# Attention block and feed-forward on one core: y turned by VectorE's 32x32 blocks and DRAM, new instruction orders

## The chip, the cores and the metric

The kernel runs on 1 core of one Trainium2 chip. The metric is the device time of one execution in microseconds (us), the slowest core's, which here is the only one; lower is better. TensorE, VectorE, ScalarE and GpSimd compute, SyncE issues DMAs. The profile calls them PE (PEld is its weight load), DVE, ACT, POOL and SP.

## What is computed

```python
x = x + layernorm(attention(layernorm(x), Wqkv, Wo))          # x is 32 batches of 256 x 128
x = x + layernorm(tanh(layernorm(x) @ w @ aux1 @ aux2 + bias))
# attention: 8 heads of 64; q and k get a positional table; causal softmax in float32
```

Below, y is the layernorm of the first sum (x1), the input of the feed-forward. All tensors are float32. The three feed-forward matrices are multiplied once, at the start, into wf.

## The kernel before

Every engine has one fixed list of instructions, written out in Python and unrolled: `begin()`, then two slots for each batch (`slot(b, 0)` and `slot(b, 1)`), then `end()`. `all_slots` (L197) calls them for batches 0 to 30; batch 31 is in `end()`. Engines meet by semaphores only, so an instruction whose semaphore isn't reached holds up everything behind it on its engine. Slots of different engines that have the same number don't run at the same time: each list says by `b.plus(n)` which batch it works on. The 8 heads are 4 pairs, named by k (half, 0 or 1) and j (pair in the half).

One batch goes through these steps:

- x: loaded (`load_x`, L218), statistics on VectorE (`stats_x`), normalised by GpSimd (`norm_x`: var_eps, rstd, minus mean, times rstd). VectorE turns its 32x32 blocks (`turn_x_blocks`, L750), SyncE sends them in four DMAs to a DRAM tensor, so placed that the whole is transposed (`send`, L240), and reads it back (`read_x`, L255). ScalarE rounds it (`keep_x_hi`, L367), VectorE takes the rest (`keep_x_lo`, L740). Batch 0 alone is transposed on TensorE.
- QK of each pair: six matmuls into the one qk_bank (`make_qk`, L974 to L976), out of which VectorE adds the positional table (`keep_qk`, L705).
- Scores (`make_scores`, L956), masked maximum on VectorE (`row_max`, L695), exp with row sums on ScalarE (`exps`, L323), reciprocal (`invert_sums`, L711). The probabilities are scaled by ScalarE (k 0, j 0), VectorE (k 1, j 0) and GpSimd (j 1, L484).
- Turning (`turn_probs`, L999) transposes the probabilities on TensorE; ScalarE keeps them (`keep_turned`, L352, L354). Both halves use the same banks.
- Vals (`make_vals`, L942 to L944) fill misc_bank, kept by ScalarE (`keep_vals`, L344). Heads (`make_heads`, L1013) are kept by VectorE (`keep_heads`, L730). Attention output (`make_attn`, L1076) uses the left half of misc_bank and is kept by ScalarE (`keep_attn`, L392).
- VectorE takes statistics and moments of the attention output, GpSimd its rstd, VectorE normalises (`norm_attn`, L679), GpSimd adds x (`make_x1`, L546), VectorE takes y's statistics and moments, GpSimd normalises y (`norm_y`, L471, L473).
- y: TensorE transposes it into the right half of misc_bank (`turn_y`, L1019), ScalarE copies it to yt (`keep_y`, L375), TensorE makes the feed-forward of it (`make_ffn`, L1047, L1049), ScalarE takes tanh (L383). The last layernorm and sum are GpSimd's (`norm_ffn`, `make_out`, L530), and SyncE stores (L261).

misc_bank is shared by vals, attention output, y and feed-forward, so each waits until the other was kept. In `end()` TensorE has `warm_up` matmuls (L1106) whose results nothing uses; 12 of them stand between the feed-forward of batch 30 and the transposes of the last y.

## Time and profile before

| | us |
|---|---|
| median of 3 runs (lowest, highest) | 536.49 (535.29, 536.52) |
| the profiled execution | 535.58 |
| its span, first to last instruction | 533.3 |
| busy PE | 508.7 (95%) |
| busy PEld | 419.7 (79%) |
| busy DVE | 458.1 (86%) |
| busy ACT | 434.5 (81%) |
| busy POOL | 394.7 (74%) |

All times in the text are of the profiled execution, from the span's start. Busy time is the time in which an engine runs at least one instruction; a pipelined matmul's end is modelled, so groups that follow each other overlap in the rows, and the distance of their starts is the better measure. In a row the instruction's start comes first, then its duration; "x12" merges twelve; in brackets stands the idle time before it and what released it.

### The profile page before, as it was taken

The numbers are of one execution on the slowest core, as the hardware profiler recorded it, in microseconds if no ns is written. First come the engines' busy times: TensorE is split into PE (matmuls) and PEld (weight loads), VectorE is DVE, ScalarE is ACT, GpSimd is POOL, SyncE is SP. The second block draws the span as 40 slices with busy tenths as digits, with TensorE's granted clock in tenths as the row PEclk, the third lists the DMA queues.
The fourth block names the chain that finished last, engine by engine and source line by source line (L and its number), as shares of the span: only waits on it lengthen the run. The fifth ranks groups of instructions, "written<-read, shape, count | busy, mean of one in ns | idle before, by whom it ended". The sixth has DMA issues, their size and how long they took to land.

```text
span 533.3 us, 17276 instructions
## 1 busy us (share of the span) xinstructions
PE 508.7 (95%) x5334; PEld 419.7 (79%) x5334; DVE 458.1 (86%) x2062; ACT 434.5 (81%) x1604; POOL 394.7 (74%) x650
## 2 busy tenths in 40 slices
PE   7689999999999999999999999999999999999984
PEld 4578888888888888888888888888888888888762
DVE  4779889988889998888999988889998889998744
ACT  2698888988888888988888888888888888889731
POOL 4434578877777887777788777778878777886654
PEclk9899999999999999999999999999999999999989
DMA  5111122111211211121121112212111221210000
GB/s 157 41 41 42 26 47 51 33 46 47 51 42 40 53 32 48 44 50 45 39 52 40 41 42 53 52 31 52 45 39 42 51 51 31 53 40 12 22 21 20
DMA packets 66223, 23.52 MB, mean 44 GB/s; under 512 B 35923, under 2 KB 65622, under 8 KB 66134
## 3 DMA queue, kind: packets, MB, share of 16 engines
q1 hardware_dynamic: 65174, 21.71, 16.9%
q8 instruction: 44, 0.72, 0.6%
q10 hardware_dynamic: 960, 0.72, 0.4%
q14 instruction: 45, 0.37, 0.3%
HBM read 14.16 MB, written 8.26 MB: 42 GB/s over the span
## 4 chain that ended last, share of the span: by engine, by line
PE 85%; issue 3%; ACT 3%; POOL 3%; DVE 3%; DMA 2%; SPq 1%; POOLq 0%; DVEq 0%; ACTq 0%
PE turned_and_heads L1013 16%; PE scores L956 15%; PE misc_bank L1076 11%; PE turned_and_heads L999 11%; PE qk_bank L974 7%; PE qk_bank L975 5%; PE qk_bank L976 5%; PE misc_bank L942 3%; PE misc_bank L943 2%; PE misc_bank L1049 2%; PE misc_bank L944 2%; PE misc_bank L1019 2%; PE misc_bank L1047 1%; DMA xt<-x_rows 1%; ACT probs L323 1%
## 5 line engine op out<-in xcount | busy, mean ns | idle before, releaser
L323 ACT ACTIVATE probs<-scores,neg_max 128x256 f32<-128x256 f32 (+1 forms) x512 | 210.2, 437 | 15.3 <-DVE neg_max L695 14.9
L695 DVE CUSTOM_DVE_ANT_0 scores<-scores,mask 128x256 f32<-128x256 f32 (+1 forms) x512 | 164.9, 385 | 7.3 <-PE scores L956 7.1
L323 ACT ACTIVATION_READ_ACCUMULATOR probs<-scores,neg_max 128x1 f32 x512 | 113.5, 222 | 0.0
L484 POOL TENSOR_TENSOR probs<-probs,inv_sum 128x512 f32<-128x512 f32 x126 | 102.8, 837 | 11.1 <-DVE inv_sum L711 11.1
L352 ACT COPY pt<-turned_and_heads 128x512 f32<-128x512 f32 x128 | 75.4, 589 | 37.8 <-PE turned_and_heads L999 37.4
L956 PE MATMUL scores<-qk 64*128 64x256 f32 (+1 forms) x1024 | 100.0, 335 | 1.1 <-ACT probs L323 1.1
L1013 PE MATMUL turned_and_heads<-pt,vals 128*64 128x256 f32 (+1 forms) x1024 | 98.5, 335 | 0.3 <-ACT pt L354 0.2
L1013 PEld LDWEIGHTS turned_and_heads<-pt,vals 128*64 128x64 f32 x1024 | 64.4, 138 | 34.7 <-issue 12.8
L956 PEld LDWEIGHTS scores<-qk 64*128 64x128 f32 x1024 | 84.7, 190 | 8.0 <-issue 1.3
L705 DVE TENSOR_TENSOR qk<-qk_bank,pe 128x512 f32<-128x512 f32 x128 | 85.7, 669 | 4.4 <-PE qk_bank L976 4.2
L974 PE MATMUL qk_bank<-xt_hi,w_hi 128*128 128x256 f32 x256 | 81.3, 318 | 4.2 <-DVE qk L705 3.4
L999 PE MATMUL turned_and_heads<-ident,probs 64*128 64x64 f32 x1536 | 75.1, 229 | 3.9 <-ACT pt L354 2.7
L999 PEld LDWEIGHTS turned_and_heads<-ident,probs 64*128 64x128 f32 x1536 | 59.6, 138 | 15.9 <-issue 11.0
L975 PE MATMUL qk_bank<-xt_lo,w_hi 128*128 128x256 f32 x256 | 71.9, 281 | 0.0
L976 PE MATMUL qk_bank<-xt_hi,w_lo 128*128 128x256 f32 x256 | 71.9, 281 | 0.0
L695 DVE DVE_READ_ACCUMULATOR2_ANT neg_max<- 128x1 f32 x512 | 69.8, 136 | 0.0
L1076 PE MATMUL misc_bank<-wo,heads_t 128*128 128x128 f32 x496 | 62.6, 279 | 3.8 <-issue 0.6
L1076 PEld LDWEIGHTS misc_bank<-wo,heads_t 128*128 128x128 f32 x496 | 57.7, 191 | 9.0 <-issue 9.0
L974 PEld LDWEIGHTS qk_bank<-xt_hi,w_hi 128*128 128x128 f32 x256 | 48.2, 188 | 14.2 <-issue 9.1
L730 DVE COPY heads_t<-turned_and_heads 128x512 f32<-128x512 f32 x64 | 44.3, 692 | 6.8 <-PE turned_and_heads L1013 4.6
L975 PEld LDWEIGHTS qk_bank<-xt_lo,w_hi 128*128 128x128 f32 x256 | 48.3, 189 | 1.3
L354 ACT COPY pt<-turned_and_heads 128x256 f32<-128x256 f32 x128 | 48.8, 381 | 0.0
(95 smaller groups left out, 905.3 us busy)
## 6 DMA issues: line engine op xcount, KB each, us to landing
x_in<-in_x SPq DMA_DIRECT2D x32, 128.0 KB, 2.3
x_res<-in_x SPq DMA_DIRECT2D x32, 128.0 KB, 2.2
out_x<-x SPq DMA_DIRECT2D x32, 128.0 KB, 2.3
x_rows<-x_blocks SPq DMA_DIRECT2D x124, 32.0 KB, 2.0
xt<-x_rows SPq DMA_DIRECT2D x31, 128.0 KB, 2.6
w_raw<-in_w_qkv_t SPq DMA_DIRECT2D x2, 256.0 KB, 4.5
w_raw<-in_w_qkv_t ACTq DMA_DIRECT2D x1, 256.0 KB, 4.4
pe<-pe_table SPq DMA_DIRECT2D x1, 256.0 KB, 5.5
```

The lines of the kernel that those rows point to most:

```text
L323: ins = nc.scalar.activation(probs[k][j][:, h, lo:hi], s_bank[j][:, h, lo:hi], ACT.Exp, bias=neg_max[k][j][:, i:i + 1], scale=-1.0, accum_ ...
L352: nc.scalar.copy(pt0[j][:, :, :].rearrange("p h (n f c) -> p (h n) f c", n=2, f=2), turned_banks[:, :, 0:T].rearrange("p f (n c) -> p n f ...
L484: ins = nc.gpsimd.tensor_tensor(some, some, inv, ALU.mult)
L695: ins = nc.vector.tensor_tensor_reduce(some, some, mask[:, t * P:2 * P], -1.0, HIGHEST, ALU.add, ALU.min, neg_max[k][j][:, i:i + 1])
L705: nc.vector.tensor_tensor(qk[j][:, :], qk_bank[:, :], pe[:, :], ALU.add).then_inc(qk_kept, 1)
L956: ins = mm(s_bank[j][:, h, at:at + k_hi], qk[j][r, q_lo:q_lo + P], qk[j][r, T:T + k_hi], start=(at == 0), stop=True, skip_group_check=True)
L974: mm(to, w_hi[:, f], hi[:, :], start=True, stop=False)
L975: mm(to, w_hi[:, f], lo[:, :], start=False, stop=False)
L976: ins = mm(to, w_lo[:, f], hi[:, :], start=False, stop=True)
L999: ins = nc.tensor.transpose(turned_banks[:, f, n * D:(n + 1) * D], some[r, h, lo:lo + P], ident[r, r])
L1013: ins = mm(heads_bank[h * D:(h + 1) * D, to], vals[b.parity][:, s, f:f + D], rhs[j][:, h, :], start=(s == 0), stop=(s == 1))
L1076: ins = mm(misc_bank[:, t * E:(t + 1) * E], heads_t[b.parity][:, p, t * P:(t + 1) * P], wo[:, p, :], start=(p == 0), stop=(p == PAIRS - 1))
```

## The change

y is no longer transposed by TensorE and copied by ScalarE. VectorE turns its 32x32 blocks (`turn_y_blocks`) from yn into y_blocks, SyncE sends them in four DMAs to a DRAM tensor y_rows (`send_y`) and reads the whole back to yt (`read_y`). Only the last batch's y goes by TensorE as before (`turn_y_last`, `keep_y_last`). The feed-forward of batch b stands one slot later in TensorE's list; it waits for y_moved and for the kept attention output of batch b + 1. All engines' slots and ends have new orders. Batches 0 to 2 have lists of their own in `begin()`, so `all_slots` starts at batch 3. In them batch 1's x too is transposed by TensorE (`turn_x`), and on VectorE the statistics of batch 1 come ahead of the first weight rest. SyncE's read_x moves to the first slot, behind both sends; load_res comes later, and each batch has 5 more DMAs.

The diff, cut (indentation shortened by twelve):

```diff
@@ all_slots
-for b in range(0, 4):
+for b in range(3, 4):
     for k in range(2):
         slot(Batch(b // 2, b % 2, B), k)
@@ sync: send_x, read_x, send_y, read_y, slot
 def send_x(b):
-    if not b.exists() or b.is_below(1):
-        return
-    sp.wait_ge(x_blocked, b.times(1))
+    if not b.exists() or b.is_below(2):
+        return
+    sp.wait_ge(x_blocked, b.times(1, -1))
     send(b, x_blocks, x_rows, x_sent)
 def read_x(b):
-    if not b.exists() or b.is_below(1):
-        return
-    sp.wait_ge(x_sent[b.parity], moves(b, 1) * 64)
+    if not b.exists() or b.is_below(2):
+        return
+    sp.wait_ge(x_sent[b.parity], moves(b, 2) * 64)
     sp.dma_start(xt[b.parity][:, :, :], x_rows[b.parity]).then_inc(x_moved[b.parity], 16)
+def send_y(b):
+    if not b.exists() or not b.plus(1).exists():
+        return
+    sp.wait_ge(y_blocked, b.times(1, 1))
+    send(b, y_blocks, y_rows, y_sent)
+def read_y(b):
+    if not b.exists() or not b.plus(1).exists():
+        return
+    sp.wait_ge(y_sent[b.parity], moves(b, 0) * 64)
+    sp.dma_start(yt[b.parity][:, :], y_rows[b.parity].rearrange("p t e -> p (t e)")).then_inc(y_moved[b.parity], 16)
 def store(b):
     if not b.exists():
...
 def slot(b, k):
     if k == 0:
         load_x(b.plus(3))
+        read_y(b.plus(-3))
+        load_res(b.plus(-1))
         send_x(b.plus(2))
+        send_y(b.plus(-2))
+        read_x(b.plus(2))
     else:
-        read_x(b.plus(2))
         store(b.plus(-3))
-        load_res(b.plus(1))
@@ scalar: keep_x_hi, keep_y, slot
 def keep_x_hi(b):
     if not b.exists():
         return
-    if b.is_first():
-        act.wait_ge(x_turned, 1)
+    if b.is_below(2):
+        act.wait_ge(x_turned, b.times(1, 1))
     else:
-        wait_moved(act, b, x_moved, 1)
+        wait_moved(act, b, x_moved, 2)
     wait(act, qk_made, pairs(b, -2, 0))
     wait(act, vals_made, b.times(2, -2))
-    nc.scalar.copy(xt_hi[b.parity][:, :], misc_bank[:, 0:T] if b.is_first() else turned_x(b)
+    nc.scalar.copy(xt_hi[b.parity][:, :], misc_bank[:, 0:T] if b.is_below(2) else turned_x(b)
                    ).then_inc(x_hi_kept, 1)
-def keep_y(b):
...
+def keep_y_last():
+    act.wait_ge(y_turned, 1)
+    act.wait_ge(ffn_made, B - 2)
+    nc.scalar.copy(yt[1][:, :], misc_bank[:, T:2 * T]).then_inc(y_kept, 1)
 def slot(b, k):
     if k == 0:
-        tanh(b.plus(-3))
+        keep_vals(b.plus(-1), 0)
+        exps(b.plus(-1), 1, 1)
+        keep_turned(b.plus(-1), 0, 0)
+        keep_vals(b.plus(-1), 1)
+        keep_turned(b.plus(-1), 0, 1)
         exps(b, 0, 0)
         keep_attn(b.plus(-2))
         exps(b, 0, 1)
+        keep_x_hi(b.plus(1))
+        keep_turned(b.plus(-1), 1, 0)
+        scale_probs(b)
     else:
-        keep_x_hi(b.plus(1))
-        scale_probs(b)
-        keep_turned(b.plus(-1), 1, 0)
-        keep_vals(b, 0)
+        tanh(b.plus(-3))
         keep_turned(b.plus(-1), 1, 1)
         exps(b, 1, 0)
-        keep_vals(b, 1)
-        exps(b, 1, 1)
-        keep_turned(b, 0, 0)
-        keep_y(b.plus(-2))
-        keep_turned(b, 0, 1)
...
@@ gpsimd: norm_y, slot
-    wait(pool, y_turned, b.times(1, -1))
+    wait(pool, y_blocked, b.times(1, -1))
 def slot(b, k):
     if k == 0:
+        rstd_attn(b.plus(-2))
         make_x1(b.plus(-2))
         norm_x(b.plus(2))
         norm_y(b.plus(-2))
+    else:
         scale_probs(b, 0)
-    else:
         norm_ffn(b.plus(-3))
         make_out(b.plus(-3))
         scale_probs(b, 1)
-        rstd_attn(b.plus(-1))
@@ gpsimd: end
 def end():
+    rstd_attn(last.plus(-2))
     make_x1(last.plus(-2))
     norm_y(last.plus(-2))
     scale_probs(last, 0)
     norm_ffn(last.plus(-3))
+    make_out(last.plus(-3))
+    rstd_attn(last.plus(-1))
+    make_x1(last.plus(-1))
+    norm_y(last.plus(-1))
     norm_ffn(last.plus(-2))
-    rstd_attn(last.plus(-1))
-    make_out(last.plus(-3))
-    make_x1(last.plus(-1))
     make_out(last.plus(-2))
-    norm_y(last.plus(-1))
     rstd_attn(last)
     rstd_y(last)
     norm_ffn(last.plus(-1))
     make_out(last.plus(-1))
     rstd_ffn(last)
 all_slots(pool, slot, begin, end)
@@ vector: turn_y_blocks, slot
+def turn_y_blocks(b):
+    if not b.exists() or not b.plus(1).exists():
+        return
+    dve.wait_ge(norms["y"]["normed"], b.times(1, 1))
+    if not b.is_below(2):
+        wait_moved(dve, b.plus(-2), y_moved, 0)
+    nc.vector.transpose(y_blocks[b.parity][:, :, :], yn[b.parity][:, :, :]).then_inc(y_blocked, 1)
 def slot(b, k):
     if k == 0:
+        scale_probs(b.plus(-1))
+        stats_x(b.plus(2))
+        turn_y_blocks(b.plus(-3))
+        row_max(b, 0, 0)
         invert_sums(b.plus(-1), 1, 1)
-        row_max(b, 0, 0)
         row_max(b, 0, 1)
         keep_qk(b, 1, 0)
-        stats_ffn(b.plus(-3))
+        wait_stats("x", b.plus(2))
         stats_attn(b.plus(-2))
+        take_moments("x", b.plus(2))
+        wait_stats("attn", b.plus(-2))
+        keep_heads(b.plus(-1), 0)
+        take_moments("attn", b.plus(-2))
         invert_sums(b, 0, 0)
-        wait_stats("attn", b.plus(-2))
-        stats_x(b.plus(2))
-        take_moments("attn", b.plus(-2))
     else:
-        wait_stats("x", b.plus(2))
-        keep_heads(b.plus(-1), 0)
-        take_moments("x", b.plus(2))
+        keep_qk(b, 1, 1)
         norm_attn(b.plus(-2))
-        keep_qk(b, 1, 1)
-        invert_sums(b, 0, 1)
         keep_x_lo(b.plus(1))
+        row_max(b, 1, 0)
         stats_y(b.plus(-2))
         wait_stats("y", b.plus(-2))
-        row_max(b, 1, 0)
+        invert_sums(b, 0, 1)
         take_moments("y", b.plus(-2))
+        stats_ffn(b.plus(-3))
         keep_qk(b.plus(1), 0, 0)
         row_max(b, 1, 1)
+        wait_stats("ffn", b.plus(-3))
         invert_sums(b, 1, 0)
-        wait_stats("ffn", b.plus(-3))
+        take_moments("ffn", b.plus(-3))
         keep_heads(b.plus(-1), 1)
-        take_moments("ffn", b.plus(-3))
         turn_x_blocks(b.plus(2))
         keep_qk(b.plus(1), 0, 1)
-        scale_probs(b)
@@ vector: begin, first part
 def begin():
     stats_x(first)
-    wait_stats("x", first)
-    take_moments("x", first)
+    moments("x", first)
     norm_first()
+    stats_x(first.plus(1))
+    moments("x", first.plus(1))
     take_w_rest(0)
     keep_x_lo(first)
     take_w_rest(1)
-    stats_x(first.plus(1))
-    wait_stats("x", first.plus(1))
-    take_moments("x", first.plus(1))
     take_w_rest(2)
-    dve.wait_ge(pe_in, 16)
     keep_qk(first, 0, 0)
+    stats_x(first.plus(2))
+    moments("x", first.plus(2))
+    keep_x_lo(first.plus(1))
     keep_qk(first, 0, 1)
     keep_fused(0)
+    row_max(first, 0, 0)
+    keep_qk(first, 1, 0)
+    row_max(first, 0, 1)
     keep_fused(1)
-    turn_x_blocks(first.plus(1))
-    dve.wait_ge(mask_in, 16)
+    keep_qk(first, 1, 1)
+    invert_sums(first, 0, 0)
+    stats_x(first.plus(3))
+    turn_x_blocks(first.plus(2))
+    row_max(first, 1, 0)
+    invert_sums(first, 0, 1)
+    keep_qk(first.plus(1), 0, 0)
...
@@ tensor: make_vals, make_ffn, slot
+    if b.is_below(3) and t == 0:
+        wait(pe_eng, vals_kept, b.times(2))
+    if b.is_first() and t == 0:
+        pe_eng.wait_ge(w_hi_made, 3)
+        pe_eng.wait_ge(w_lo_made, 3)
     if t == 0:
         wait(pe_eng, attn_kept, b.times(1, -1))
         wait(pe_eng, tanh_done, b.times(1, -2))
-        pe_eng.wait_ge(x_lo_kept, b.times(1, 1))
-        wait(pe_eng, y_kept, b.times(1, -2))
+        pe_eng.wait_ge(x_lo_kept, 2 if b.is_first() else b.times(1, 1))
     else:
         pe_eng.wait_ge(vals_kept, b.times(2, 1))
     hi, lo = xt_hi[b.parity][:, t * P:(t + 1) * P], xt_lo[b.parity][:, t * P:(t + 1) * P]
...
-    pe_eng.wait_ge(y_kept, b.times(1, 1))
+    if b.plus(1).exists():
+        wait_moved(pe_eng, b, y_moved, 0)
+    else:
+        pe_eng.wait_ge(y_kept, 1)
+    if b.plus(2).exists():
+        pe_eng.wait_ge(attn_kept, b.times(1, 2))
+    else:
+        pe_eng.wait_ge(attn_kept, B - 1)
+        pe_eng.wait_ge(tanh_done, b.times(1))
     mm(misc_bank[:, T:2 * T], part_ones[:, :], bias_parts[:, :], start=True, stop=False, skip_group_check=True)
 def slot(b, k):
     if k == 0:
-        make_qk(b, 1, 1)
-        turn_probs(b.plus(-1), 1, 0)
-        make_scores(b, 1)
-        turn_probs(b.plus(-1), 1, 1)
-        make_qk(b.plus(1), 0, 0)
-        make_vals(b, 1)
-        make_heads(b.plus(-1), 1)
-        make_qk(b.plus(1), 0, 1)
-    else:
-        turn_y(b.plus(-2))
-        turn_probs(b, 0, 0)
-        make_scores(b.plus(1), 0)
-        turn_probs(b, 0, 1)
-        make_ffn(b.plus(-2))
-        make_qk(b.plus(1), 1, 0)
         make_attn(b.plus(-1), 0)
         make_attn(b.plus(-1), 1)
+        make_qk(b.plus(1), 1, 0)
         make_heads(b, 0)
+        make_qk(b.plus(1), 1, 1)
+        turn_probs(b, 1, 0)
+        make_scores(b.plus(1), 1)
+        turn_probs(b, 1, 1)
+    else:
+        make_ffn(b.plus(-2))
+        make_qk(b.plus(2), 0, 0)
         make_vals(b.plus(1), 0)
+        make_heads(b, 1)
+        make_qk(b.plus(2), 0, 1)
+        make_vals(b.plus(1), 1)
+        turn_probs(b.plus(1), 0, 0)
+        make_scores(b.plus(2), 0)
+        turn_probs(b.plus(1), 0, 1)
@@ tensor: begin, first part
+    turn_x(first)
     warm_up(7, qk_bank)
     make_qk(first, 0, 0)
-    pe_eng.wait_ge(w_hi_made, 3)
-    pe_eng.wait_ge(w_lo_made, 3)
+    turn_x(first.plus(1))
+    make_qk(first, 0, 1)
+    fuse(0)
+    make_scores(first, 0)
+    make_qk(first, 1, 0)
+    fuse(1)
     make_vals(first, 0)
-    make_qk(first, 0, 1)
-    pe_eng.wait_ge(ffn_in, 16 * 3)
-    fuse(0, w2_sb, w1t_sb)
-    make_scores(first, 0)
-    pe_eng.wait_ge(fused_dve, 1)
-    fuse(1, w12t_sb, w3_sb)
-    make_qk(first, 1, 0)
+    make_qk(first, 1, 1)
+    make_vals(first, 1)
+    make_scores(first, 1)
+    make_qk(first.plus(1), 0, 0)
+    turn_probs(first, 0, 0)
+    make_qk(first.plus(1), 0, 1)
+    make_vals(first.plus(1), 0)
+    turn_probs(first, 0, 1)
+    make_scores(first.plus(1), 0)
+    make_qk(first.plus(1), 1, 0)
...
@@ tensor: end
 def end():
-    turn_probs(last.plus(-1), 1, 0)
-    make_qk(last, 1, 1)
-    make_vals(last, 1)
-    turn_probs(last.plus(-1), 1, 1)
-    make_scores(last, 1)
-    make_heads(last.plus(-1), 1)
-    turn_y(last.plus(-2))
-    turn_probs(last, 0, 0)
-    make_ffn(last.plus(-2))
-    turn_probs(last, 0, 1)
     make_attn(last.plus(-1), 0)
     make_attn(last.plus(-1), 1)
     warm_up(4, qk_bank, 256)
     make_heads(last, 0)
     warm_up(4, qk_bank, 256)
     turn_probs(last, 1, 0)
+    make_ffn(last.plus(-2))
     turn_probs(last, 1, 1)
     warm_up(4, qk_bank, 256)
     make_heads(last, 1)
     pe_eng.wait_ge(exps_done, 4 * B)
     warm_up(3, s_bank[0][:, 0, :])
     make_attn_last()
-    turn_y(last.plus(-1))
     make_ffn(last.plus(-1))
     warm_up(12, s_bank[0][:, 0, :])
-    turn_y(last)
+    turn_y_last()
     warm_up(4, s_bank[0][:, 0, :], 256)
     make_ffn(last)
 all_slots(pe_eng, slot, begin, end)
```

## Rows read from the trace of the kernel before

**Rows 1.** Busy time in one batch: us; PE, PEld, DVE, ACT, POOL; PEclk, DMA, GB/s.
```profile
265.46:280.92 15.46, 15.34 (x167) 12.86 (x165) 14.05 (x65) 13.45 (x51) 12.43 (x20) 1.00 0.19 45
```

**Rows 2.** Timeline of PE from 271 to 281 us.
```profile
271.65 0.28 PE L976 MATMUL qk_bank<-xt_hi,w_lo 128*128 128x256 f32 x1
271.77 0.44 PE L1019 MATMUL misc_bank<-ident,yn 128*128 128x128 f32 x2
272.14 0.59 PE L999 MATMUL turned_and_heads<-ident,probs 64*128 64x64 f32 x12
...
275.62 0.28 PE L976 MATMUL qk_bank<-xt_hi,w_lo 128*128 128x256 f32 x1
276.03 2.02 PE L1076 MATMUL misc_bank<-wo,heads_t 128*128 128x128 f32 x16
277.98 1.52 PE L1013 MATMUL turned_and_heads<-pt,vals 128*64 128x256 f32 x16
...
280.00 0.39 PE L944 MATMUL misc_bank<-w_hi,xt_lo 128*128 128x512 f32 x1
280.23 0.28 PE L974 MATMUL qk_bank<-xt_hi,w_hi 128*128 128x256 f32 x1
```

**Rows 3.** Timeline of PE in the first 60 us.
```profile
17.98 0.36 PE L974 MATMUL qk_bank<-xt_hi,w_hi 128*128 128x256 f32 x1 [3.16 <-DVE qk L705]
...
40.66 0.56 PE L999 MATMUL turned_and_heads<-ident,probs 64*128 64x64 f32 x11
...
55.21 0.59 PE L999 MATMUL turned_and_heads<-ident,probs 64*128 64x64 f32 x12
```

**Rows 4.** Timeline of POOL and PE in the last 20 us.
```profile
518.36 0.20 POOL L461 TENSOR_TENSOR y_var_eps<-y_moments,eps 128x2 f32<-128x2 f32 x1 [3.03 <-DVE y_moments L644]
...
522.31 2.75 PE L1106 MATMUL scores<-warm 128*128 128x512 bf16 x12
...
525.90 0.44 PE L1019 MATMUL misc_bank<-ident,yn 128*128 128x128 f32 x2 [0.83 <-DVE yn L808]
```

**Rows 5.** Timeline of PE from 499 to 507 us.
```profile
499.27 0.40 PE L944 MATMUL misc_bank<-w_hi,xt_lo 128*128 128x512 f32 x1
499.60 0.59 PE L999 MATMUL turned_and_heads<-ident,probs 64*128 64x64 f32 x12
...
505.79 0.59 PE L999 MATMUL turned_and_heads<-ident,probs 64*128 64x64 f32 x12 [0.47 <-ACT pt L354]
506.31 0.94 PE L1076 MATMUL misc_bank<-wo,heads_t 128*128 128x128 f32 x6
```

**Rows 6.** Timeline of DVE and of POOL from 262.5 to 275 us.
```profile
263.96 0.23 DVE L644 BATCH_NORM_AGGREGATE attn_moments<-attn_stats 128x2 f32<-128x6 f32 x2
...
271.67 1.61 POOL L484 TENSOR_TENSOR probs<-probs,inv_sum 128x512 f32<-128x512 f32 x2
```

**Rows 7.** Waits of DVE (total us, times, longest), and its 31 block transposes.
```profile
DVE attn_stats L631 <- ACT attn L392: 24.9, 31, 1.1
DVE attn_n L679 <- POOL attn_rstd L464: 10.8, 31, 0.7
...
L750 DVE STREAM_TRANSPOSE x_blocks<-xn 128x256 f32<-128x256 f32 x31 | 12.8, 414 | 0.0
```

**Rows 8.** DMA issues, landing of xt's reads, and SP's four sends.
```profile
x_rows<-x_blocks SPq DMA_DIRECT2D x124, 32.0 KB, 2.0
...
DMA to landing us min/median/max: 1.9/2.6/4.2
...
272.32 2.55 SPq L240 DMA_DIRECT2D x_rows<-x_blocks  x4
```

**Rows 9.** Timeline of DVE and of ACT in the first 22 us.
```profile
8.85 0.49 DVE L631 BATCH_NORM_STATS2 x_stats<-x_in 128x6 f32<-128x128 f32 x2 [0.69 <-DMA x_in<-in_x]
...
20.90 0.41 ACT L367 CAST xt_hi<-xt 128x256 fp32r<-128x256 f32 x1 [1.50 <-DMA xt<-x_rows]
```

**Rows 10.** The page's costliest groups: exps on ACT (busy us, mean ns, idle before).
```profile
L323 ACT ACTIVATE probs<-scores,neg_max 128x256 f32<-128x256 f32 (+1 forms) x512 | 210.2, 437 | 15.3 <-DVE neg_max L695 14.9
```

262 lines of the change are left out of this document (200 added, 62 removed).

## The prediction

> **What bounds the kernel now.** I read the page's busy shares first, then the busy time of one batch, then TensorE's instructions over one batch, then the waits, and last the first 60 and the last 30 us. TensorE leads with 95% of the span (the table above), and within one batch of the middle it is busy 15.34 of 15.46 us at full granted clock [rows 1]. What the reader is to see in its timeline [rows 2] is that each group starts where the one before it ends: a batch lasts 15.47 us, and from the first turning of batch 2 (55.21) [rows 3] to that of batch 16 (272.14) a batch takes 216.93 / 14 = 15.50 us, hiccups included. So in the middle only TensorE's own list counts, unless another chain becomes as long. VectorE is next: 14.05 us of a batch [rows 1], plus the waits it cannot avoid. The ends are different: TensorE stands idle there, and chains set the time [rows 3, 4].
>
> **Steady state, TensorE's list.** A batch keeps the same groups, less the two transposes of y. They cost no more than their place in the list: from the last matmul of the first half's second QK group (271.65) to the transposes 0.12 us, from them to the next turning 0.37 [rows 2]. Neighbours change too, so I count each step from a group's last matmul (or its start, where its length does not change) to the next group. Steps that go: QK to turned y 0.12, turned y to turning 0.37, QK to attention output 0.41 (276.03 less 275.62), vals to QK 0.23 (280.23 less 280.00) [rows 2]; sum 1.13. Steps that come: vals to turning, 0.33, and turning to attention output, 0.52, within the 0.59 that a turning itself lasts, so nothing is lost there [rows 5]. QK to heads and QK to the first half of vals have no row. Each has three waits; QK to a group whose wait is over costs 0.12, QK to attention output with its four waits 0.41. I take 0.25 for each, between the two, as three waits are nearer to four than to none but at least one is long over. So 1.13 is replaced by 0.33 + 0.50 = 0.83: 0.30 less a batch, 15.20 us. Bounds 0.56 less (both 0.12) and 0.02 more (both 0.41).
>
> **Steady state, the chains beside it.** The new lists are tight, so I follow three loops. (1) Heads of the first half, kept by VectorE 1.57 us after they begin (length 1.52 and a hand-over of 0.05) [rows 2], 0.61 of VectorE until the moments of the attention output, then from those moments through rstd, norm_attn, x1, norm_x and norm_y to GpSimd's scaling 7.71 (263.96 to 271.67), the scaling 1.61, turning 0.52, attention output 1.95, QK 0.8 and 0.25: 15.0 us [rows 2, 5, 6]. Before, this chain hung on the attention output and had about 0.6 to spare; now it hangs on the heads and is 0.2 short of TensorE. (2) VectorE: 14.05 + 0.41 for turning y's blocks + the wait inside its own list between the moments and norm_attn, 10.8 / 31 = 0.35: 14.8 us [rows 1, 7]. Its other wait, 24.9 / 31 = 0.8 for the kept attention output [rows 7], must shrink to what is left, 0.4. (3) The round trip of y. SyncE issues 13 DMAs a batch instead of 8. An issue of send takes 0.65 (2.55 for four), so its queue fills about 7.5 us, with read_x now behind both sends and read_y behind store and load_x. From VectorE's turn: 0.41, four issues 2.6, flight 2.0, read 2.6 = 7.6 us until y has moved [rows 7, 8]. The room for it: VectorE keeps the heads 1.57 after they begin; of its 14.8 us the turn of y, two row maxima, a kept QK, one stats, one moments and one inversion (0.36 + 2.5 + 0.6 + 0.4 + 0.2 + 0.1 = 4.1) lie between that turn and the next heads, so the turn is 1.57 + 10.7 = 12.3 after the heads' start. The feed-forward is 4.8 after the heads of its slot (heads 1.45, QK 1.0, turning 0.42, scores 1.38, turning 0.52), so 15.2 + 4.8 - 12.3 = 7.7 us after the turn. The trip just fits, and what is late by e costs e/2 a batch, since this loop spans two batches. ScalarE loses y's copy, but is busy 13.45 only and gains nothing for the end. With all three loops within 0.1 to 0.4 of TensorE's 15.20 I take 15.30 a batch: 0.20 less, over the 27 batches from 3 to 29, **-5.3 us**. From -10 (15.13) to +1.
>
> One rule speaks against moving a transpose off TensorE: the Trainium skill, "VectorE: DVE Perf Modes", Rules for kernel authors, would leave a 128x128 transpose on TensorE where PSUM may take it. The rows above say that here TensorE has no room and VectorE has 0.4 us, so the rule would give 0 for the steady state and my sum -5.3.
>
> **The start.** Now the first turning of batch 1 is at 40.66 [rows 3]. TensorE idled 3.16 us up to 17.98, because VectorE took both row maxima before it kept a QK [rows 3], and batch 1's x came by DRAM, with ScalarE idle 1.50 for it [rows 9]. The new lists put a keep_qk between the maxima and turn batch 1's x on TensorE. Against that, VectorE's statistics of batch 1 now stand ahead of the first weight rest. Their data lands at 8.85 only [rows 9], so the first QK result is kept some 2 us later than now, at about 12.2. From there I walk the lists: first scores 13.8 to 15.3, their first row maximum 14.8 to 16.0, exps to 17.7 (four activations of 0.437 mean, overlapping to 1.6) [rows 10], then a kept half of vals, the second exps 18.2 to 19.8 behind its maximum, scaling 1.5, first turning 21.9. Then ScalarE holds the pace: exps of the second half to 23.4, keep_turned 0.75, exps to 25.8, so the next scores end at 26.5; behind them QK, heads, vals, QK, turning, scores, turning, QK, a short wait for keep_turned (33.7), heads, QK, half an attention output and scores follow (0.9 + 1.5 + 0.7 + 0.8 + 0.5 + 1.4 + 0.5 + 0.8 + 0.2 + 1.5 + 0.8 + 1.0 + 1.4 = 12.0) to 38.5 for the turning of batch 1. One score group (1.4) and half an attention output (1.0) are by then done that now come later: 40.66 + 2.4 - 38.5 = 4.6 gained. A walk has no friction; I take **-3.8**. Bounds -5 and +1 (nothing gained but the late start kept).
>
> **The end.** y of batch 30 must cross DRAM too, and in TensorE's list its feed-forward and 12 warm-up matmuls stand ahead of the last y. Its moments were taken late (GpSimd idle 3.03 until 518.36) [rows 4]; now they are taken at once and GpSimd normalises it earlier, so I put the normed y at 516.5. Add 7.6 for the trip: 524.1, 0.6 of feed-forward and 2.6 of warm-up (2.75 with the last one's tail, from 522.31): the last y is turned at 527.3 instead of 525.90, +1.4 [rows 4]. The front of the tail gains 0.4 (one turning of y less). **+1.0**, from -0.5 to +2.7.
>
> **Sum.** The profiled execution took 535.58 us with 533.3 us of span. 535.58 - 5.3 - 3.8 + 1.0 = 527.5 us. The median of the runs, 536.49, is 0.9 above the profiled one; I do not add that. A change under 0.3% (1.6 us) is about what a measurement of this kernel cannot tell from none.
>
> **Rivals.** (A) *The steps on TensorE cost what the old ones did*: the waits of heads and vals show in full (0.41 each), or TensorE waits 0.2 for keep_heads, now only one QK behind the heads. The middle stays at 15.50, start and end as above: 532.8 us. For it: the loops leave 0.2. 20%. (B) *y is late, slower than before*: feed-forward waits for y's read in every batch. It decides from the point where the loop of two batches passes 31.0 + 0.2, that is where y comes some 0.9 us later than forecast. The sends of x and y now share the rings, and both sends and the read could be slower: reads landed after 1.9 to 4.2 us [rows 8]. With 1.5 us more the batch is 15.15 + 0.75 = 15.9: 27 x 0.4 = +10.8, with start and end 543.5 us. Against it: 32 KB sends land in 2.0 us, less than a 128 KB read. 12%. The Trainium skill, "DMA: Bandwidth & Descriptors", Why small descriptors are slow (HBM only), names small pieces as slow, and y's sends are made of them. The same send of x lands in 2.0 us in the row, so the trace so far does not bear the rule out. (C) *VectorE becomes the bound*: its extra 0.41 and a worse fit of waits (it has 0.4 us) eat the middle's gain and 2 us of the start: 535 us, no difference. 10%. (D) *No loop binds and the new steps cost 0.12*: 15.1 a batch, 522 us. 8%. The forecast itself: 50%, its own range 524 to 531.
>
> Faster: forecast, A, D = 0.78. Same: C = 0.10. Slower: B = 0.12. The range goes from 523, which leaves out most of D, to 536, which leaves out B.
>
> **What would show it.** In the changed profile the two transposes of y are gone from the middle, the vals to turning step is 0.33 and QK to heads and to vals about 0.25. First turnings of successive batches are 15.3 us apart. VectorE is busy 14.4 us of that, and 31 turns of y's blocks of 0.41 stand there. TensorE's longest releaser in the middle is none, or VectorE's kept heads. A wait of feed-forward for the DMA of y of more than 0.3 us a batch means B. The first turning of batch 1 near 38.5, the last y turned 1 to 1.5 us later within the tail. A period over 15.45, or a start later than 41, would make the forecast wrong.

## The result and the profile after

| | us |
|---|---|
| kernel after, median of 7 runs (lowest, highest) | 538.63 (535.86, 541.39) |
| kernel before, beside it, 7 runs | 536.12 (534.65, 536.69) |
| ratio, 95% interval | 1.0048 [1.0026, 1.0070] |
| profiled execution after, and its span | 536.81, 534.6 |

The change makes the kernel 0.5% slower, where I forecast 527.5 us. The profiled execution is 1.8 us below the median: it is a good one of its kind, and this matters below.

The page of the kernel after: busy times, packets, and the chain that ended last (shares of the span by engine).

```profile
PE 502.0 (94%) x5274; PEld 413.6 (77%) x5274; DVE 470.8 (88%) x2092; ACT 427.6 (80%) x1573; POOL 395.3 (74%) x650
DMA packets 103184, 31.40 MB, mean 59 GB/s; under 512 B 69043, under 2 KB 102582, under 8 KB 103094
PE 51%; DVE 16%; SPq 9%; issue 8%; DMA 7%; ACT 5%; POOL 3%; POOLq 0%; DVEq 0%; ACTq 0%
```

TensorE has 6.7 us less work than before (508.7), as meant, and yet the end comes no earlier. The last line tells why: it held 85% of the chain before and holds 51% now, and SyncE's queue and DMAs, 3% before, have 16%. Something on SyncE is now in the way.

One batch of the middle, in the columns of [rows 1]: it lasts longer than one before (15.46), but TensorE is busy for 15.07 of it, not 15.34 (15.08 of 15.64 in the batch ahead of it).

```profile
271.57:287.39 15.82, 15.07 (x164) 12.62 (x163) 14.43 (x66) 13.21 (x52) 12.75 (x21) 1.00 0.28 60
```

The same batch on four engines. VectorE turns x's blocks and, 2.7 us later, y's:

```profile
270.83 0.44 DVE L812 STREAM_TRANSPOSE x_blocks<-xn 128x256 f32<-128x256 f32 x1
...
273.57 0.42 DVE L821 STREAM_TRANSPOSE y_blocks<-yn 128x256 f32<-128x256 f32 x1
```

SyncE issues what follows from that, one thing behind the other:

```profile
271.30 2.55 SPq L242 DMA_DIRECT2D x_rows<-x_blocks  x4
274.02 3.85 SPq L242 DMA_DIRECT2D y_rows<-y_blocks  x4
277.92 0.60 SPq L257 DMA_DIRECT2D xt<-x_rows  x1
```

ScalarE waits for x, and TensorE for the copy that stands behind that wait:

```profile
280.28 0.41 ACT L386 CAST xt_hi<-xt 128x256 fp32r<-128x256 f32 x1 [1.34 <-DMA xt<-x_rows]
280.60 0.58 ACT L371 COPY pt<-turned_and_heads 128x512 f32<-128x512 f32 x1
```

```profile
279.54 1.56 PE L1086 MATMUL scores<-qk 64*128 64x256 f32 x16
281.70 0.59 PE L1129 MATMUL turned_and_heads<-ident,probs 64*128 64x64 f32 x12 [0.60 <-ACT pt L373]
```

The last of x's four sends is issued at 273.24 and landed at 275.22. Their read is issued at 277.92, because y's four sends are ahead of it in the queue. Over the run it looks like this (waits: total us, times, longest):

```profile
ACT xt_hi L386 <- DMA xt<-x_rows: 16.7, 20, 1.4
...
PE turned_and_heads L1129 <- ACT pt L373: 6.9, 13, 1.2
...
PEld misc_bank L1180 <- DMA yt<-y_rows: 6.0, 8, 3.9
```

Before, the first of these waits was 1.9 us, twice. The middle as a whole is read from the first turning of batch 3 and that of batch 30, before and after:

```profile
70.59 0.28 PE L999 MATMUL turned_and_heads<-ident,probs 64*128 64x64 f32 x2
...
489.15 0.28 PE L999 MATMUL turned_and_heads<-ident,probs 64*128 64x64 f32 x2
```

```profile
69.83 0.28 PE L1129 MATMUL turned_and_heads<-ident,probs 64*128 64x64 f32 x2
...
488.77 0.28 PE L1129 MATMUL turned_and_heads<-ident,probs 64*128 64x64 f32 x2
```

27 batches took 418.56 us and take 418.94: 15.50 and 15.52 each. The start gained 0.76 in these two profiles. The tail, from the turning of batch 30 to the end of the span, took 533.3 - 489.15 = 44.15 and takes 534.6 - 488.77 = 45.83: 1.7 lost.

The start, which I had put 3.8 us faster. VectorE waits for batch 1's x with the weights' rests behind it, so the first QK comes at 10.86; then TensorE waits for that x again, with the second QK behind it:

```profile
9.13 0.49 DVE L689 BATCH_NORM_STATS2 x_stats<-x_in 128x6 f32<-128x128 f32 x2 [3.49 <-DMA x_in<-in_x]
```

```profile
10.86 0.39 PE L1104 MATMUL qk_bank<-xt_hi,w_hi 128*128 128x256 f32 x1 [2.71 <-DVE xt_lo L802]
...
13.22 0.33 PE L1149 MATMUL misc_bank<-ident,xn 128*128 128x128 f32 x1 [1.07 <-POOL xn L520]
...
24.33 0.28 PE L1129 MATMUL turned_and_heads<-ident,probs 64*128 64x64 f32 x2
...
41.69 0.28 PE L1129 MATMUL turned_and_heads<-ident,probs 64*128 64x64 f32 x4
```

The tail: y of batch 30 is sent and read, TensorE waits for it, and 12 warm-up matmuls stand between its feed-forward and the last y. They take 3.65 us now and took 2.75 before [rows 4]: behind the wait of 3.68 us TensorE was granted half its clock, 1.2 GHz, for 3.4 us (0.77 and 0.81 in the two windows of 4 us, third from the end of the row; 1.00 in both before).

```profile
516.09 2.54 SPq L242 DMA_DIRECT2D y_rows<-y_blocks  x4
...
520.73 0.34 SPq L272 DMA_DIRECT2D yt<-y_rows  x1
```

```profile
522.70 0.40 PE L1180 MATMUL misc_bank<-bias_parts,part_ones 128*128 128x256 bf16 x1 [3.68 <-DMA yt<-y_rows]
...
523.74 3.65 PE L1238 MATMUL scores<-warm 128*128 128x512 bf16 x12
527.22 0.38 PE L1149 MATMUL misc_bank<-ident,yn 128*128 128x128 f32 x2
```

```profile
520.00:524.00 4.00, 1.30 (x6) 1.14 (x7) 1.77 (x7) 0.02 (x1) 1.69 (x4) 0.77 0.21 66
524.00:528.00 4.00, 4.00 (x18) 1.83 (x16) 1.26 (x6) 0.73 (x2) 2.24 (x5) 0.81 0.00 0
```

### The profile page after: what moved, and what is told of

Its sections match the earlier page's. It is cut to its first block, busy times and chain, and to the rows that moved or that the text cites. A ratio compares the mean times of both kernels' runs of the same rounds, so it can differ in the third digit from the quotient of the medians.

```text
span 534.6 us, 17330 instructions
## 1 busy us (share of the span) xinstructions
PE 502.0 (94%) x5274; PEld 413.6 (77%) x5274; DVE 470.8 (88%) x2092; ACT 427.6 (80%) x1573; POOL 395.3 (74%) x650
## 4 chain that ended last, share of the span: by engine, by line
PE 51%; DVE 16%; SPq 9%; issue 8%; DMA 7%; ACT 5%; POOL 3%; POOLq 0%; DVEq 0%; ACTq 0%
PE turned_and_heads L1143 11%; SPq L242 8%; PE scores L1086 8%; PE misc_bank L1209 7%; PE turned_and_heads L1129 7%; DMA xt<-x_rows 4%; PE qk_bank L1104 4%; DVE scores L755 4%; PE qk_bank L1105 3%; PE qk_bank L1106 3%; DVE qk L767 2%; PE misc_bank L1182 2%; PE misc_bank L1072 2%; DVE probs L783 2%; PE misc_bank L1073 2%
## 5 line engine op out<-in xcount | busy, mean ns | idle before, releaser
L531 POOL TENSOR_TENSOR probs<-probs,inv_sum 128x512 f32<-128x512 f32 x126 | 111.1, 902 | 20.3 <-DVE inv_sum L773 20.3
L342 ACT ACTIVATION_READ_ACCUMULATOR probs<-scores,neg_max 128x1 f32 x512 | 117.8, 230 | 0.0
L1143 PE MATMUL turned_and_heads<-pt,vals 128*64 128x256 f32 (+1 forms) x1024 | 97.3, 332 | 0.9 <-ACT pt L373 0.7
L1086 PEld LDWEIGHTS scores<-qk 64*128 64x128 f32 x1024 | 87.8, 190 | 4.7 <-issue 0.8
L1129 PE MATMUL turned_and_heads<-ident,probs 64*128 64x64 f32 x1536 | 75.2, 229 | 13.5 <-ACT pt L373 6.9
L1104 PE MATMUL qk_bank<-xt_hi,w_hi 128*128 128x256 f32 x256 | 84.0, 328 | 3.6 <-DVE xt_lo L802 2.7
L755 DVE DVE_READ_ACCUMULATOR2_ANT neg_max<- 128x1 f32 x512 | 71.0, 139 | 0.0
L1209 PE MATMUL misc_bank<-wo,heads_t 128*128 128x128 f32 x496 | 63.7, 281 | 0.1
L783 DVE TENSOR_TENSOR probs<-probs,inv_sum 128x512 f32<-128x512 f32 x64 | 49.3, 809 | 0.1
```

Of the source, the lines that this page charges most:

```text
L342: ins = nc.scalar.activation(probs[k][j][:, h, lo:hi], s_bank[j][:, h, lo:hi], ACT.Exp, bias=neg_max[k][j][:, i:i + 1], scale=-1.0, accum_ ...
L531: ins = nc.gpsimd.tensor_tensor(some, some, inv, ALU.mult)
L755: ins = nc.vector.tensor_tensor_reduce(some, some, mask[:, t * P:2 * P], -1.0, HIGHEST, ALU.add, ALU.min, neg_max[k][j][:, i:i + 1])
L1086: ins = mm(s_bank[j][:, h, at:at + k_hi], qk[j][r, q_lo:q_lo + P], qk[j][r, T:T + k_hi], start=(at == 0), stop=True, skip_group_check=True)
L1104: mm(to, w_hi[:, f], hi[:, :], start=True, stop=False)
L1129: ins = nc.tensor.transpose(turned_banks[:, f, n * D:(n + 1) * D], some[r, h, lo:lo + P], ident[r, r])
```

## The experiments

All are edits of the kernel after. "Period" is the distance of the first turnings of batches 3 and 30 in the profiled execution, divided by 27. Ratios are to runs of the kernel before made beside them (medians 535.5 to 536.1).

| run | median us | ratio [95%] | period |
|---|---|---|---|
| no_trip | 530.82 | 0.9902 [0.9876, 0.9928] | 15.33 |
| trip_unused | 537.28 | 1.0033 [1.0015, 1.0050] | 15.52 |
| x_hi_later | 544.43 | 1.0157 [1.0131, 1.0182] | 15.74 |
| start_stats_later | 539.62 | 1.0067 [1.0045, 1.0089] | 15.65 |
| x_turn_earlier | 539.76 | 1.0071 [1.0049, 1.0093] | 15.55 |
| plain_sends | 532.35 | 0.9936 [0.9913, 0.9959] | 15.34 |
| tail_warm_first | 538.11 | 1.0046 [1.0025, 1.0067] | 15.67 |
| start_x1_later | 539.71 | 1.0067 [1.0044, 1.0090] | 15.62 |
| sp_order | 535.16 | 0.9990 [0.9968, 1.0012] | 15.42 |
| y_read_first | 539.39 | 1.0068 [1.0047, 1.0089] | 15.51 |
| start_warm | 540.94 | 1.0091 [1.0060, 1.0121] | 15.75 |
| all_three | 533.07 | 0.9955 [0.9935, 0.9976] | 15.36 |
| no_trip_scale_first | 525.68 | 0.9805 [0.9788, 0.9822] | 15.15 |
| three_scale_first | 531.80 | 0.9915 [0.9890, 0.9940] | 15.43 |
| three_start | 530.74 | 0.9893 [0.9873, 0.9912] | 15.45 |
| three_act_send | 530.30 | 0.9888 [0.9872, 0.9905] | 15.33 |
| all_one_send | 525.45 | 0.9794 [0.9771, 0.9816] | 15.26 |
| all_two_sends | 531.59 | 0.9913 [0.9894, 0.9932] | 15.44 |

Four of these runs leave the middle as it is in the kernel after (start_stats_later, tail_warm_first, start_x1_later, start_warm). Their profiles show 15.62 to 15.75, but these executions took 0.5 to 3.6 us more than the medians of their own runs, as the one with 15.52 took 1.8 less. If all of that lay in the middle, the five would come to 15.57 to 15.62 (an estimate). Without the trip it is 15.33, in an execution 0.3 above its median. So periods of single profiles tell differences of 0.2, but hardly of 0.1.

**no_trip**: the trip taken out, the blocks used as they are.

```diff
 def slot(b, k):
-    read_y(b.plus(-3))
-    send_y(b.plus(-2))
...
-    wait_moved(pe_eng, b, y_moved, 0)
+    pe_eng.wait_ge(y_blocked, b.times(1, 1))
...
-    ins = mm(misc_bank[:, T + t * E:T + (t + 1) * E], yt[b.parity][:, t * P:(t + 1) * P], wf[:, :],
+    y = y_blocks[b.parity][:, t, :] if b.plus(1).exists() else yt[1][:, t * P:(t + 1) * P]
+    ins = mm(misc_bank[:, T + t * E:T + (t + 1) * E], y, wf[:, :],
```

> Left out: y's 32x32 blocks are not brought through DRAM (no sends, no read), and the feed-forward of batches 0 to 30 multiplies the blocks as VectorE left them, as soon as they are turned. SyncE issues 8 DMAs a batch again. Theory (the trip through SyncE's queue costs the middle its gain): the first turnings of successive batches come 15.05 to 15.15 us apart instead of 15.52, which is 10 to 12.5 us over 27 batches, and the tail loses the 3.7 us wait for the read of batch 30's y, of which 2 to 3 remain as gain: 521 to 525 us. Rival (VectorE, or its kept heads, bounds the middle; the trip is hidden): the period stays at 15.4 to 15.5 and only the tail gains: 532 to 535 us.

530.8 us, 7.8 under the kernel after and between the two ranges. So the trip costs 8 us: 1.4 in the tail (44.45 against 45.83) and the rest, about 6.4, in the middle. The period without it is 15.33, not the 15.1 that I expected from this theory: something else holds the middle there, very evenly. From the last score matmul to the second turning TensorE takes 0.35 instead of 0.11, as GpSimd's scaling ends at 302.53 only; it takes 2.06 us where it took 1.61 before [rows 6]:

```profile
300.47 2.06 POOL L529 TENSOR_TENSOR probs<-probs,inv_sum 128x512 f32<-128x512 f32 x2
```

```profile
301.07 1.53 PE L1084 MATMUL scores<-qk 64*128 64x256 f32 x16
302.68 0.53 PE L1127 MATMUL turned_and_heads<-ident,probs 64*128 64x64 f32 x10
```

**trip_unused**: as no_trip, but SyncE sends and reads as in the kernel after; only nobody waits for yt.

> Left out: the feed-forward of batches 0 to 30 does not use y as it comes back from DRAM but the blocks as VectorE left them; the four sends and the read of y run as in the changed kernel. So nothing waits for y, but x's read still stands behind y's sends. Theory A (it is mainly x that comes late, because its read is queued behind y's sends, and ScalarE's rounding of x blocks the turned probabilities): the period stays over 15.3, 529 to 534 us, 5 or more above the kernel without the trip. Theory B (it is the wait of the feed-forward for y): within 2 us of the kernel without the trip, 522 to 526 us.

537.3 us and 15.52, above both ranges, which were set from a kernel without the trip at 521 to 525. Against the 530.8 that it has, 6.5 us are back, with the trip there but nobody waiting for y; the tail is as short as without it (44.46). It is x that is late (ScalarE waits 19.0 us for it, 25 times). Theory A's mechanism stands.

**x_hi_later**: the obvious mend, x's rounding moved behind the copy that it held up.

```diff
-    keep_x_hi(b.plus(1))
     keep_turned(b.plus(-1), 1, 0)
+    keep_x_hi(b.plus(1))
```

> ScalarE's rounding of the next batch's x stands behind its copy of the second half's first turned pair instead of ahead of it. Theory A (x late blocks that copy, and TensorE's next turning waits for it, 7.8 us over 27 batches): 3 to 6 us faster than the changed kernel, 531 to 535 us, and the wait of TensorE for the copy gone. Theory B (the late y takes the place of what is gained, since its loop is as long): within 1 us, 536 to 538 us.

A miss, 9 us above theory A's range: 544.4. ScalarE hardly waits for x any more (0.8 us), but VectorE, which takes x's rest, waits for ScalarE (7.0 us, 29 times, not at all in the kernel after), which shifts VectorE's whole list and with it the turning of y. Now the feed-forward waits for y (16.3 us, 20 times). No batch is shorter than 15.53 (15.04 in the kernel after), so this holds every batch. Both of SyncE's reads are at their limit; here what relieved one loaded the other.

**x_turn_earlier**: VectorE turns x's blocks 0.8 us earlier.

```diff
+    turn_x_blocks(b.plus(2))
     wait_stats("ffn", b.plus(-3))
     invert_sums(b, 1, 0)
     take_moments("ffn", b.plus(-3))
     keep_heads(b.plus(-1), 1)
-    turn_x_blocks(b.plus(2))
```

> VectorE turns x's blocks ahead of the inversion, ffn moments and kept heads of its slot, 0.8 us earlier; nothing else changes, so all eight sends and both reads move that much earlier on SyncE only as far as x is concerned. Theory (x's read, queued behind y's sends, reaches ScalarE too late, and this lateness is what lifts the middle from the 15.30 us of the kernel without the trip to 15.52): ScalarE's wait for x falls from 16.7 us in all to under 4, the period falls to 15.3 to 15.4, and the time to 531.5 to 534.5 us. Rival (the batches are long because the sends themselves are stretched, whatever their place in time, or because the kept heads are now 0.36 us later): 536 to 539 us.

No gain (539.8, 0.8 above the rival's range too). The wait for x is still 14.9 us: x's read stands behind y's sends, and those did not move.

**plain_sends**: the same DMAs and bytes, but y's sends put whole rows down.

```diff
+    if blocks is y_blocks:
+        sp.dma_start(to[b.parity][r, :, :], blocks[b.parity][r, :, :]).then_inc(sent[b.parity], 16)
+        continue
```

> Left out: the four sends of y put whole rows of 512 B into DRAM instead of 32x32 blocks in rows of 128 B, so y is not transposed across blocks. The DMAs, their number, bytes and order on SyncE stay. Theory A (SyncE's order and number of issues set the wait): issues still take 0.6 each, x is as late as before, and the time stays within 1.5 us of the changed kernel, 535.5 to 538.5. Theory B (the small pieces do it: the rings fill and an issue is stretched to 1 to 2 us): the stretched issues vanish, ScalarE's wait for x falls below 6 us, and the time falls to 531 to 534 us.

532.4 us, 6.3 of the 7.8 that the trip costs, and ScalarE's wait for x is 2.3 us: theory B has the better of it. But its mechanism is only half right. The stretched issues stay (20 of over 0.75 us between 70 and 485 us, 19 in the kernel after), though they sit elsewhere: 4 of them are y's sends and 8 the read of x, where 12 were y's sends. What falls is the ordinary issue. Minimum, median and longest issue in ns, after and with plain rows:

```profile
L242 SPq DMA_DIRECT2D y_rows<-y_blocks x124: 569/611/1958, 57.1 to 518.0; - x124
```

```profile
L242 SPq DMA_DIRECT2D y_rows<-y_blocks x124: 312/421/1665, 54.9 to 510.4; - x124
DMA packets 75408, 31.40 MB, mean 59 GB/s; under 512 B 37299, under 2 KB 74806, under 8 KB 75318
```

Four issues are 0.8 us shorter, and with 0.4 less flight the read of y starts 1.0 us sooner after the turn (medians 4.3 and 5.3). The Trainium skill, "DMA: Bandwidth & Descriptors", Why small descriptors are slow (HBM only), speaks of a cost of each small piece in the transfer itself. These runs bear out that small pieces cost, and add that of the 1.0 us by which the read comes sooner some 0.8 can be put down to the issues, on the engine that issues.

**sp_order and y_read_first**: SyncE's order. sp_order is this; y_read_first moves read_y alone.

```diff
     load_x(b.plus(3))
-    read_y(b.plus(-3))
     load_res(b.plus(-1))
     send_x(b.plus(2))
-    send_y(b.plus(-2))
+    send_y(b.plus(-2), range(2))
     read_x(b.plus(2))
+    send_y(b.plus(-2), range(2, 4))
+    read_y(b.plus(-2))
```

> SyncE issues four sends of x, two of y, the read of x, two of y, the read of y, and only then the store and the loads; nothing else is changed. x's read is issued 1.3 us earlier, y's read 0.4 earlier. Theory (SyncE's queue makes both reads about 1 us too late for the middle, and y's small-piece sends are what fills it): ScalarE's wait for x falls from 16.7 us to under 6, the period from 15.52 to 15.30 to 15.40, the time to 532 to 535 us. Rival (the flights of x's and y's blocks delay each other whatever the order of issue, or y takes over as the late one): 536 to 539 us.

> SyncE reads y right behind the read of x, ahead of the store and of the next x's load; x's read stays where it is. So y lands up to 1 us earlier, x when it did. Theory (the late x is the larger part: 7.8 us of TensorE's excess against 1.8 at the feed-forward): a gain of under 2 us, 536 to 538.5 us, with ScalarE's wait for x still over 14 us. Rival (the late y is what counts, and x's lateness follows from it): 532 to 535 us.

sp_order: 535.2 us, 3.5 under the kernel after, just outside the theory's range, as is the period (15.42); x's wait is gone and y's is what is left.

```profile
PE misc_bank L1181 <- DMA yt<-y_rows: 8.6, 11, 4.3
...
ACT xt_hi L387 <- DMA xt<-x_rows: 0.5, 1, 0.5
```

y_read_first: 539.4, no gain, x's wait 19.4 us. Its upper bound of 538.5 was missed, its mechanism (x is the larger part) held.

**no_trip_scale_first and three_scale_first**: is the remaining 15.33 GpSimd's chain? y's normalisation goes behind the first scaling; the first of them has no trip, the second is all_three (below) with this edit.

```diff
     norm_x(b.plus(2))
-    norm_y(b.plus(-2))
 else:
     scale_probs(b, 0)
+    norm_y(b.plus(-2))
```

> Left out as in the kernel without the trip: y's blocks are not brought through DRAM. GpSimd normalises y behind its first scaling instead of ahead of it. Theory (the 15.30 us of the kernel without the trip is the chain from the kept heads over GpSimd to its scaling, the first loop of the forecast): TensorE's 0.35 us wait ahead of the second turning goes, the period falls to 15.05 to 15.1, the time to 523.5 to 526 us. Rival (VectorE is the bound, or y is then late for its turn): 529 to 531 us, period 15.3.

> The kernel with the three changes (SyncE's order, warm-ups at the start and at the end), and GpSimd normalises y behind its first scaling. y is ready before VectorE turns it even so (302.5 against 303.1 us in one batch), so y's trip starts no later. Theory (what is left over 15.05 a batch in that kernel, 0.25, is half GpSimd's chain and half the late y): 530 to 532 us. Rival (y's own lateness takes its place, since a faster batch leaves the trip less time): 532.5 to 534.5 us.

525.7 us and 15.15: it is. The second turning now follows the scores at once.

```profile
297.44 1.53 PE L1084 MATMUL scores<-qk 64*128 64x256 f32 x16
298.81 0.59 PE L1127 MATMUL turned_and_heads<-ident,probs 64*128 64x64 f32 x12
```

With the trip there (three_scale_first) the median is 1.3 us under all_three's, but the intervals overlap; its period is no shorter, as two batches met a late y, and one of them a slower clock too (last section). Neither of its theories is settled by it.

**start_stats_later, start_warm, start_x1_later, three_start**: the start. The first puts batch 1's statistics back behind the third weight rest. The second has 16 warm-ups for 7. The third has the edit below, and VectorE's statistics of batches 1 and 2 moved to fit; three_start besides moves what else stood in the way, and has the new SyncE order and the tail's edit. What makes these profiles hard to compare is TensorE's granted clock, which fell to 1.2 GHz for 3.4 or 6.8 us in some of them and not in others (last section); I say it for each.

```diff
     make_qk(first, 0, 0)
-    turn_x(first.plus(1))
     make_qk(first, 0, 1)
     fuse(0)
     make_scores(first, 0)
+    turn_x(first.plus(1))
```

> VectorE takes the statistics of batch 1 behind the third part of the weights' rest again, as before the change. Theory (in the changed kernel VectorE waits 3.5 us for batch 1's x at 9.13 with the first weight rests behind that wait, and TensorE's first QK starts at 10.86 instead of 7.51): first QK near 7.6, first turning of batch 0 at 22 instead of 24.3, and 1.5 to 3 us faster in all, 534 to 535.5 us. Rival (the statistics of batch 1 are then late for its own turning, or ScalarE holds the pace anyway): first turning of batch 1 stays at 41.5 to 41.9, and the time within 1 us of the changed kernel.

The first QK comes at 7.36, as expected, but behind the second TensorE waits 3.59 us for batch 1's x (12.63), and the clock was 1.2 GHz for 6.8 us from 11.7 on: first turning at 24.81, nothing gained.

> 16 warm-up matmuls instead of 7 ahead of the first QK. Theory (TensorE's idle 2.7 us ahead of its first QK is what drops its clock to 1.2 GHz between 12 and 18 us: in the run with plain sends the clock stayed at 2.4 GHz, and its first turning came at 22.1 us instead of 24.3 to 25.8): the granted clock is 1.00 from 8 to 24 us, the first turning comes at 22.0 to 23.0, that of batch 3 1.5 to 2.5 us earlier, 534.5 to 536.5 us. Rival (the first turning varies with the landing of the inputs): 24 us or more as before, no change in the time within 1 us.

A miss. The first turning came at 23.67, within the spread of the ten kernels with the start unchanged (22.10 to 25.77), and the clock fell all the same (0.64 from 12 to 14 us, 0.50 to 16). The run as a whole was slower, for no cause that I can name in the start; the middle of this profile is told in the last section.

> TensorE transposes batch 1's x behind the first scores instead of ahead of the second QK, and VectorE takes its statistics after it has kept the first QK; its rest of x comes behind the first row maximum. Theory (batch 1's x lands at 9.0 us, its normalisation ends at 12.6, and TensorE, VectorE and all behind them wait for that at the start): first scores at 12.3 to 12.8 instead of 15.3, first turning of batch 0 at 21.5 to 22.8 instead of 24.3, first turning of batch 3 1.5 to 2.5 us earlier, 534.3 to 535.5 us. Rival (ScalarE's exps, vals and copies hold the pace behind the start): the first turning moves, that of batch 3 by under 0.5 us, and the time stays at 536 to 537.5.

First turning at 21.74, as forecast by that theory, but batch 1's at 41.74: VectorE stood 1.99 us for GpSimd to normalise batch 2's x, whose statistics now came late, TensorE stood 2.01 us behind it, and then had 1.2 GHz for 3.4 us. A rival that I had named in general, at a place I had not seen; the time (539.7) is above its range as well.

> SyncE's order and the tail's warm-ups as in the kernel with the three changes; at the start 7 warm-ups as in the changed kernel, batch 1's x transposed behind the first scores, its statistics behind the first kept QK, and the statistics of batch 3 and the turning of batch 2's x behind batch 0's third row maximum and the first kept QK of batch 1. Theory (batch 1's x holds up the start): first turning of batch 0 at 21.5 to 22, that of batch 1 at 38.8 to 39.8 instead of 41.6, and 531 to 532.5 us. Rival (ScalarE and VectorE take up the gain before batch 1 is turned, as when batch 2's statistics were in the way): first turning of batch 1 at 41 or later, 533 to 534.5 us.

With that mended:

```profile
20.10 0.31 PE L1130 MATMUL turned_and_heads<-ident,probs 64*128 64x64 f32 x3
...
39.07 0.22 PE L1130 MATMUL turned_and_heads<-ident,probs 64*128 64x64 f32 x2
```

Batch 1 is turned at 39.07 (38.5 was the forecast for the changed kernel), 2.6 earlier than after, and all_three less this is 2.3 us. But the clock did not fall here. three_scale_first, with the old order, batch 1's x as late as here (8.9) and no fall either, turned batch 1 at 40.00, so of the 2.6 us the order by itself explains 0.9, and most of the rest is clock. The three kernels with this start all kept the clock, of the ten with the old one nine did not: that the new order is what keeps it is likely, and not shown.

**tail_warm_first, all_three, three_act_send**. The first moves the 12 warm-ups ahead of the feed-forward of batch 30. The second joins it with sp_order and start_warm. The third is the second with one send moved to ScalarE.

```diff
 # ScalarE, slot k = 0
     keep_turned(b.plus(-1), 0, 1)
+    send_last_y(b.plus(-3))
     exps(b, 0, 0)
```

> The 12 warm-up matmuls of the tail stand ahead of the feed-forward of batch 30 instead of behind it. Theory (the 3.7 us in which TensorE waits for that batch's y, then the 3.5 us of warm-up behind it, set when the last y is turned, 527.22): the warm-up runs in the wait, the last y is turned when it is normed, near 524.9, and the run is 2 to 2.7 us shorter, 534 to 535 us. Rival (the end hangs on another chain, batch 30's own feed-forward through GpSimd and its store): 0 to 0.7 us shorter.

538.1 against 538.6: the medians can't tell it. In the profile the tail from the last batch's first turning to the end takes 538.5 - 509.26 = 29.24 instead of 534.6 - 503.97 = 30.63, so 1.4 gained, less than expected: TensorE still waits for y, 1.6 us now instead of 3.7, but its clock stays at 2.4 GHz until the last feed-forward. The kernels with the tail unchanged that wait for y had 1.2 GHz there for 3.4 us (five profiles, from batch 30's turning to the end 45.8 to 46.3 us) or 6.8 us (four, 47.5 to 47.9), those with this edit 44.5.

> The new order of SyncE's queue, 16 warm-up matmuls ahead of the first QK, and the tail's 12 warm-ups ahead of the feed-forward of batch 30, together. If each is worth what its theory says (middle 3 to 6, start 1.5 to 2.5, tail 1.4): 529.5 to 533 us, that is faster than both kernels. If only the tail's part holds: 536.5 to 537.5 us.

533.1, at the upper end: middle and tail gave their share, the start nothing (first turning 24.21, with the clock fallen).

> The kernel with the three changes, with the last of y's four sends issued by ScalarE between its copies and its first exps, where it waits 0.68 us for a row maximum anyway; SyncE issues seven sends a batch. Theory (SyncE's issue time is the rest of the trip's cost): both reads are issued 0.65 us earlier, the feed-forward's wait for y goes (3.9 us in excess over 27 batches), 530.5 to 532.5 us. Rival (an issue holds up ScalarE for 0.6 us in every batch and its exps are late): 533.5 to 540 us.

530.3 us, 2.8 under all_three, the best of the single steps. The feed-forward's wait for y is 2.0 us, twice. The issue costs ScalarE nothing, as it runs beside a copy and the wait that was there anyway:

```profile
302.36 0.59 ACT L372 COPY pt<-turned_and_heads 128x512 f32<-128x512 f32 x1 [0.68 <-PE turned_and_heads L1139]
302.59 0.58 ACTq L419 DMA_DIRECT2D y_rows<-y_blocks  x1
...
303.91 0.47 ACT L343 ACTIVATE probs<-scores,neg_max 128x256 f32<-128x256 f32 x1 [0.68 <-DVE neg_max L765]
```

**all_one_send, all_two_sends**: everything together, with one or two sends by ScalarE.

> All parts together: SyncE's order, the new start, GpSimd's scaling ahead of its normalisation of y, one of y's sends issued by ScalarE, the tail's warm-ups ahead of the feed-forward. If the gains add (the kernel with ScalarE's send 530.3, less 2.3 for the start, less 1.5 to 2.5 for GpSimd's order): 525.5 to 527 us, period 15.2, near the 525.7 of the kernel without the trip and with GpSimd's order. Rival (the faster middle meets the late y again): 527.5 to 530 us, with the feed-forward's wait for y over 4 us in excess.

> The same, with two of y's sends issued by ScalarE, six a batch left on SyncE. Theory (the trip still costs the middle about 0.1 us a batch with one send moved, and ScalarE's wait of 0.68 us for the row maximum hides both issues): 1 to 2 us faster than with one, 524 to 526 us, period 15.1 to 15.15. Rival (the second issue holds up ScalarE's exps, or nothing is left to gain): equal to or slower than with one.

One send: 525.5 us, ratio 0.9794, the best version, and the gains add. Two sends: 531.6, as the rival has it (slower than with one). y is in time, but the second issue took 0.90 us in this batch, and ScalarE's exps start 1.10 us after its last work instead of 0.68; over the middle 18 of ScalarE's 54 issues took more than 0.75 us, and none of the 27 with one send. The kept attention output comes later, VectorE idles ahead of its statistics (16.2 us, 24 times, against 5.0, 14 times), keeps the heads late, and TensorE waits for them (15.6 us, 28 times, against 4.5).

```profile
303.33 0.90 ACTq L419 DMA_DIRECT2D y_rows<-y_blocks  x1
304.33 0.47 ACT L343 ACTIVATE probs<-scores,neg_max 128x256 f32<-128x256 f32 x1 [1.10 <-DVE neg_max L765]
```

```profile
307.87 0.59 PE L1139 MATMUL turned_and_heads<-ident,probs 64*128 64x64 f32 x12 [0.54 <-DVE heads_t L802]
```

## Why the prediction was wrong

**TensorE's list: right.** I put it at 15.20 a batch with bounds 14.94 and 15.52. The busy time fell from 15.34 to 15.07, and the shortest batches of the kernel after last 15.04 to 15.07. The steps that had no row were a little cheaper than taken (QK to heads 0.22, QK to vals 0.12, against 0.25 each).

**The first loop, GpSimd's chain: the right place, 0.3 too small.** By the sum it was 15.0, below TensorE's 15.20; without the trip it bound the middle, at 15.33, and at 15.15 when y's normalisation was out of it. The term that was short is the scaling, 1.61 taken and 2.06 measured. The 15.30 that I took came out close because I had added 0.1 for all loops together, which is luck.

**The second loop, VectorE: right**, in that the kernel without the trip and with GpSimd's order went to 15.15 with all of VectorE's work in it.

**The third loop, the round trip: this is the step that failed, in two ways.** (1) I sized y's trip, 7.6 us against 7.7 of room, and wrote of x only that its read now stood "behind both sends". Its own sum would have been: 0.47 from the turning of x to the first issue and 0.17 between x's and y's (both as in the kernel after), 2.55 for x's four, 2.55 for y's four, and 2.6 from the read's issue to its landing [rows 8], 8.3 us. The room, which I did not work out, is no more: in the kernel without the trip ScalarE took one batch's x at 308.35, with x turned at 300.03, 8.3 us before, and 8.3 is the median there too. So x was as tight as y, and measured it lands 8.8 us after its turning (median of the 27 batches), half a microsecond late in a usual batch and over one where an issue is stretched. trip_unused, in which 6.5 us are lost by this alone, says that it is nearly the whole loss of the middle. (2) Of y the room was as forecast (the shortest time from its turn to the feed-forward is 7.63), but the trip was 8.0 in the median and 8.6 at the longest. A send's issue of 0.61 to 0.65 us is the usual one, but 19 issues in the 27 batches took over 0.75 and up to 1.96 us, which I had not looked for: the flights in [rows 8] are medians. With eight sends one behind the other, nothing absorbs it. By the medians the middle lost 6.4 us to this (7.8 less the tail's 1.4), by the estimated periods above 6.5 to 7.8, of which I had allowed for nothing.

**The start: 3 us mis-sized, half of it by the clock.** 3.8 was forecast, 0.76 came. The walk put the first scores at 13.8, the first row maximum at 14.8 and the first turning at 21.9; they came at 15.30, 17.15 and 24.33. plain_sends has the same start and met them at 13.80, 14.92 and 22.10:

```profile
15.30 2.36 PE L1086 MATMUL scores<-qk 64*128 64x256 f32 x16
```

```profile
13.80 1.58 PE L1089 MATMUL scores<-qk 64*128 64x256 f32 x16
```

Two things differ. Batch 1's x landed at 8.4 there and at 9.1 here, and the clock stayed at 2.4 GHz there and was 1.2 GHz here from 13.5 to 17.0, which stretched the scores from 1.58 to 2.36 us. three_scale_first, with x at 8.9 and no fall, turned batch 0 at 22.65. So of the 2.4 us at the first turning some 1.5 are the clock, of which the prediction says nothing, and 0.75 the order of the list: TensorE turns batch 1's x ahead of the second QK, so all waits for GpSimd to normalise it (13.22), and I had charged the late statistics to the first QK on VectorE alone. From turning 0 to turning 1 the walk had 16.6, measured 17.36. The 0.76 itself is no firm number: with the start unchanged, batch 3 was first turned at 67.64 to 71.23 in ten profiles, and the kernel before has a single one, with a fall of its own (18.8 to 22.2).

**The end: near in size, +1.0 forecast, +1.7 measured, by two errors against each other.** The last y was turned at 527.22 (forecast 527.3). But batch 30's y was there at 522.7, not 524.1, and feed-forward and warm-ups behind it then took 4.5 us instead of 3.2, because of the clock. In four of the nine profiles with this tail the clock stayed low for twice as long, and the end lost 3.3 to 3.8 us. The kernel before had a fall too, but earlier in its tail (from 513.8 to 517.2).

**Sum.** For the profiled execution 527.5 + 5.8 (middle, 418.94 less 27 x 15.30) + 3.0 (start) + 0.7 (end) = 537.0, with 536.81 measured; the median, 538.63, lies 1.8 higher, and where those lie one profile can't say.

Of the rivals B had the right place, the queue and the sends, but the wrong victim: it looked for a late y of 1.5 us. Its row, the landing after 2.0 us, was no evidence against it, since most of the price of the small pieces lies in the issue, and the row of four issues (2.55) stood beside it.

**Where the expected gain went:** off TensorE and into waits for SyncE's queue. all_one_send is 2.1% faster than the kernel before [0.9771, 0.9816], 10.6 us, and 13.2 under the kernel after. Step by step, as if the medians of the runs added, 3.5 of the 13.2 are SyncE's order, 2.8 the send that ScalarE issues, 2.3 the new start and 2.1 the warm-ups of start and tail; the rest, 2.5, is left for GpSimd's order. So 6.3 came out of the queue.

## What to carry to other kernels

When an edit adds DMAs to one queue, write out the queue's whole list for one period, with the issue times, and give each read in it its own deadline, that of the old traffic first: what becomes late is what stands behind the new work, not the new work itself. A loop that "just fits" with 0.1 us of room by medians doesn't fit, because a stretched issue (19 in 27 batches here), not the median one, decides. A DMA's issue can move to an engine with a wait that is there anyway, but only as much of it as that wait holds: one send gained 2.8 us, and a second one cost 6. And before a start or a tail is compared between two profiles, look at the granted clock in both: here it was worth 1.5 us at the start and 1 to 3 at the end.

## What the runs showed of the hardware that I had not expected

The issue of a 32 KB send takes longer in small pieces: 611 ns against 421 with whole rows of 512 B, while the flight differs by 0.4 us. Issues of over 0.75 us, most of them of 1 to 2 us, come in all kernels looked at (6 of 214 between 70 and 485 us in the kernel before, 8 of 214 without the trip, 19 of 348 with it, 20 of 350 with whole rows), more often with more DMAs in the queue, and their cause stays open.

A stall can cost more than its length, through TensorE's clock, and doesn't always. In start_warm TensorE waited 1.84 us for ScalarE's copy ahead of 314.89, and 1.81 us ahead of 364.03. Up to the end of the waits it had been busy for 6.02 and 6.04 of 8 us. The granted clock, third from the end of the row (columns of [rows 1]), then was 0.59, and 0.56 in the next 2 us, that is 1.2 GHz for 3.4 us; the other time it stayed at 1.00. The first batch took 18.57 us, the second 17.27.

```profile
308.00:316.00 8.00, 6.02 (x74) 5.01 (x73) 6.07 (x29) 5.47 (x22) 5.60 (x10) 1.00 0.39 97
316.00:318.00 2.00, 2.00 (x11) 1.60 (x9) 1.61 (x7) 1.85 (x8) 1.40 (x3) 0.59 0.00 0
```

```profile
358.00:366.00 8.00, 6.04 (x74) 5.25 (x71) 5.82 (x28) 5.53 (x21) 5.36 (x11) 1.00 0.35 91
366.00:368.00 2.00, 2.00 (x19) 1.25 (x18) 2.00 (x11) 2.00 (x11) 1.78 (x4) 1.00 0.00 0
```

In three_scale_first a batch took 18.52 us in the same way: a read of y was issued only 9.8 us into it, TensorE waited 1.82 us, and the clock was 0.59 and 0.55 in the 4 us behind.

At the start the clock is the same kind of lottery. Of ten kernels whose start is that of the kernel after, nine fell to 1.2 GHz between 10 and 20 us, for 3.4 or 6.8 us, and turned batch 0 at 23.9 to 25.8; the tenth, plain_sends, kept 2.4 GHz and turned it at 22.10. With 16 warm-ups it fell in three of four, with the start of three_start in none of three. The window from 14 to 16 us, after and with plain sends:

```profile
14.00:16.00 2.00, 2.00 (x11) 1.69 (x12) 1.35 (x4) 0.07 (x1) 1.70 (x5) 0.50 0.22 66
```

```profile
14.00:16.00 2.00, 2.00 (x21) 1.79 (x20) 1.67 (x9) 0.00 (x0) 1.73 (x5) 1.00 0.05 13
```

TensorE does 11 matmuls at the one and 21 at the other. What decides between them stays open.
